# The end of a fused four-layer kernel: experts merged beside the norms, and half of each tile's experts scaled and added by two other engines

## The reference, cut to what matters

```python
# the closing norm of the fourth cross attention; its result is added to x
out = (out - mu) * jax.lax.rsqrt(var + EPS) * ln_scale + ln_bias      # EPS = 1e-6
x = x + out
# the encoder runs on _layernorm(x), which has no scale of its own
def _moe(x, wg, w1, b1, w2, b2):               # 8 experts, D = 128, FF = 512
    xf = x.reshape(S, D)                       # S = 2048 tokens, cap = S // 8
    gates = jax.nn.softmax(xf @ wg, axis=-1)
    idx = jnp.argmax(gates, axis=-1)
    ... # loc: the token's place among those of its expert; keep = loc < cap
    h = jnp.einsum('ecd,edf->ecf', disp, w1) + b1[:, None, :]
    y = (jnp.einsum('ecf,efd->ecd', h, w2) + b2[:, None, :]).reshape(E * cap, D)
    out = jnp.where(keep[:, None], gate_val[:, None] * y[...], 0.0)
y1 = _ln(x + _mha(x, in_proj_w, in_proj_b, out_proj_w, out_proj_b), ln1_g, ln1_b)
y2 = _ln(y1 + _moe(y1, wg, w1, b1, w2, b2), ln2_g, ln2_b)
x = x + y2                                     # the kernel's output
```

## Time and profile before

| what | value |
|---|---|
| median of three runs | 4094.75 us |
| the profiled execution's own time | 4094.75 us |
| its span in the profile | 4093.0 us |
| PE busy | 3629.6 us (89%) |
| DVE busy | 2716.3 us (66%) |
| ACT busy | 2253.7 us (55%) |
| POOL busy | 1367.2 us (33%) |

### The profile page before, as it was taken

How to read it: one execution, slowest core, us unless ns; L and a number is a source line. 1 busy time by engine, 2 the same in 40 slices (tenths; PEclk the granted TensorE clock), 3 DMA queues, 4 the chain that set the end, 5 groups by cost and what they waited for, 6 DMA issues and landing times. The chain is left out here.

```text
span 4093.0 us, 72451 instructions
## 1 busy us (share of the span) xinstructions
PE 3629.6 (89%) x28012; PEld 2243.5 (55%) x28017; DVE 2716.3 (66%) x4497; ACT 2253.7 (55%) x3885; POOL 1367.2 (33%) x1655
## 2 busy tenths in 40 slices
PE   3699999889699986997889999999999999999554
PEld 2233333478444434675457776777677776776441
DVE  5799999644477736554347666666666666766648
ACT  2599999633277752222146566665666566656220
POOL 3011111230011102210035556655565556556310
PEclk7699999999799986998989999999999999999777
DMA  4422232001256401000010000000000000000010
GB/s 140 130 59 54 49 58 48 21 12 36 65 78 92 67 2 31 2 2 10 12 53 17 1 1 17 1 17 1 17 1 17 1 17 1 1 1 1 7 42 16
DMA packets 117717, 122.90 MB, mean 30 GB/s; under 512 B 19008, under 2 KB 95648, under 8 KB 116992
## 3 DMA queue, kind: packets, MB, share of 16 engines
q1 hardware_dynamic: 104184, 111.20, 12.0%
q10 hardware_dynamic: 13200, 7.16, 0.6%
HBM read 102.51 MB, written 15.68 MB: 29 GB/s over the span
## 5 line engine op out<-in xcount | busy, mean ns | idle before, releaser
L869 DVE TENSOR_REDUCE att_peak.1<-psS 128x1 f32<-128x512 f32 (+1 forms) x1024 | 579.1, 633 | 21.0 <-PE psS L744 14.7
L2098 DVE TENSOR_TENSOR att_highest.1<-att_highest.1,psS 128x1024 f32<-128x1024 f32 (+1 forms) x320 | 356.7, 1115 | 218.1 <-ACT prob_0.1 L2032 111.8
L839 ACT ACTIVATE att_probT.1<-psT 128x512 f32<-128x512 f32 (+1 forms) x682 | 366.6, 568 | 29.6 <-PE psT L773 9.6
L2190 POOL TENSOR_TENSOR key_sums_0.1<-key_sums_0.1,prob_0.1 128x512 f32<-128x512 f32 x256 | 334.5, 1306 | 28.7 <-POOL key_sums_0.1 L2190 0.4
L2190 POOL TENSOR_TENSOR key_sums_1.1<-key_sums_1.1,prob_1.1 128x512 f32<-128x512 f32 x256 | 332.3, 1298 | 32.8 <-ACT prob_1.1 L2038 5.1
L869 DVE TENSOR_REDUCE att_peak.2<-psS 128x1 f32<-128x512 f32 (+1 forms) x512 | 261.7, 568 | 79.1 <-PE psS L744 76.2
L790 PE MATMUL psM<-att_probT.1,quad_values.1 128*9 128x256 f32 (+1 forms) x3840 | 292.6, 382 | 0.2 <-issue 0.2
L744 PE MATMUL psS<-key_stack.1,query_stack.1 64*128 64x512 bf16 (+1 forms) x1024 | 253.6, 379 | 25.0 <-PEq L379 15.9
L2110 DVE TENSOR_REDUCE att_shift.4<-psO 128x4 f32<-128x512 f32 x64 | 44.3, 692 | 319.0 <-PE psO L1941 319.0
L2185 POOL TENSOR_TENSOR key_sums_0.1<-prob_0.1 128x512 f32<-128x512 f32 x64 | 81.8, 1277 | 517.2 <-ACT prob_0.1 L2038 517.2
L2119 DVE TENSOR_TENSOR prob_1.1<-prob_1.1,psO 128x1024 f32<-128x1024 f32 (+1 forms) x256 | 245.7, 1012 | 5.6 <-PE psO L1948 5.6
(11 more groups left out here) (687 smaller groups left out, 7857.2 us busy)
## 6 DMA issues: line engine op xcount, KB each, us to landing
key_stack.1<-key_parts SPq DMA_DIRECT2D x384, 58.0 KB
key_stack.2<-key_parts SPq DMA_DIRECT2D x96, 200.1 KB
ctx_rows.1<-in_ctx_dram SPq DMA_DIRECT2D x8, 1536.0 KB
key_parts<-split_parts.2 SPq DMA_DIRECT2D x8, 1200.8 KB, 7.4
ctx_keys_0.1<-in_ctx_dram ACTq DMA_DIRECT2D x4, 768.0 KB
ctx_keys_1.1<-in_ctx_dram ACTq DMA_DIRECT2D x4, 768.0 KB
query_stack.1<-query_parts SPq DMA_DIRECT2D x192, 16.0 KB
ctx_values_0.1<-in_ctx_dram SPq DMA_DIRECT2D x4, 768.0 KB
```

Of the source, the lines that this page charges most:

```text
L839: self.k.nc.scalar.activation(probs[:, blks[0]:blks[-1] + 1, :].rearrange("p b q -> p (b q)"), bank[0:w, 0:len(blks) * S], ACT.Exp).then_i ...
L869: self.k.nc.vector.tensor_reduce(self.peak[:, 2 * h + s, c:c + 1], self.score_bank[m % 3][:, 0:w], AX_X, ALU.max).then_inc(self.peak_done. ...
L2098: self.k.nc.vector.tensor_tensor(own, old, new, ALU.max).then_inc(self.raised.sem, 1)
L2190: nc.gpsimd.tensor_tensor(acc, acc, own[:, h, c * BANK:(c + 1) * BANK], ALU.add).then_inc(self.summed.sem, 1)
```

## The change

The new code is in seven parts.

- `MergedExperts` keeps all weights of the eight experts in buffers of their own and the merged result in `both[P, E, 2, D]`: for each expert the matrix and its bias row. The bias row gets `b2` by a matmul with a row of ones, and the bias product is the same on every partition.
- `two_norms_beside_experts` joins the closing norm of the cross attention, its scale and shift, and the norm ahead of the encoder in one block. DVE goes by groups of four tiles. SP issues the loads of the experts (25 DMAs) and those of scale and shift, ACT the eleven others, and PE, ACT and POOL merge experts 0 to 3.
- `norm_beside_experts` does ln1, its scale and shift, and the transposes in one block, and merges experts 4 to 7 on the other engines; on PE they stand ahead of the transposes.
- The blocks `load` and the loop over the experts are gone; `softmax_gates` and `place_in_order` stay.
- `apply_experts` adds the bias rows on PE, by a matmul with one row of contraction (the ones times the bias rows) into the same PSUM bank. DVE takes experts 0 to 3 straight from PSUM. ACT scales experts 4 to 7 by the token's weight into a ring of three buffers, POOL adds the four to one, and DVE adds that one two tiles later and takes the tile's statistics for ln2 at once.
- `last_norm` does the rest of ln2 by groups of four tiles, and SP stores each group (256 KB).
- `scale_and_shift`, `transpose_tokens`, `single_expert` and `store` are gone.

```diff
+def dve_scale_and_shift(k, link, norm, g, scale, shift):
+    for t in range(4 * g, 4 * g + 4):
+        last = norm.dve_apply(t)
+    link(last)
+    x = four_tiles(k.XN, g)
+    link(k.nc.vector.tensor_tensor(x, x, over_four(scale), ALU.mult))
+    return k.nc.vector.tensor_tensor(x, x, over_four(shift), ALU.add)
...
+    def pe_run(self, pe, first, end):            # MergedExperts
+        self.pe_turn(pe, first)                  # 4 transposes of w1
+        for e in range(first, end):
+            if e + 1 < end:
+                self.pe_turn(pe, e + 1)
+            self.pe_product(pe, e)               # 4 + 4 + 1 matmuls
...
+        @block.sync                              # two_norms_beside_experts
+        def _(sp):
+            for e in range(2):
+                experts.load(sp, e)
+            for dst, src in ((scale, "L3_xattn_ln_scale"), (shift, "L3_xattn_ln_bias")):
+                sp.dma_start(dst[:], rows(k.dram[src])).then_inc(affine_loaded.sem, 16)
+            for e in range(2, E):
+                experts.load(sp, e)
+            sp.wait_ge(*loaded(16 * len(loads)))
...
+            old.dve_invert(dve, link)
+            dve.wait_ge(*affine_loaded(32))
+            for g in range(NT // 4):
+                link(dve_scale_and_shift(k, link, old, g, scale, shift))
+                x = four_tiles(k.X, g)
+                link(nc.vector.tensor_tensor(x, x, four_tiles(k.XN, g), ALU.add))
+                for t in range(4 * g, 4 * g + 4):
+                    last = new.dve_stats(t)
...
+        def _(pe):                               # norm_beside_experts
+            experts.pe_run(pe, EARLY, E)         # EARLY = 4
+            for g in range(NT // 4):
+                pe.wait_ge(*xn_done(g + 1))
+                turn_tiles(k, pe, g, xt_done)
...
-                for i in range(HALF):            # apply_experts, PE
-                    n = t * HALF + i
-                    if n >= 4:
-                        pe.wait_ge(*biased(n - 3))
-                    nc.tensor.matmul(k.psS[:, n % 4, :], k.XT[:, t * P:(t + 1) * P], w12[:, i * BANK:(i + 1) * BANK],
-                                     start=True, stop=True).then_inc(product.sem, 1)
+                for i in range(2):
+                    if t >= 2 and i == 0:
+                        pe.wait_ge(*added(added_at(t - 2)))
+                    if t >= 2 and i == 1:
+                        pe.wait_ge(*scaled(EB * (t - 1)))
+                    own = slice(EB * i, EB * i + EB)
+                    out = k.psS[:, 2 * i + t % 2, :].rearrange("p (e d) -> p e d", d=D)
+                    nc.tensor.matmul(out, k.XT[:, t * P:(t + 1) * P], experts.both[:, own, 0, :], start=True, stop=False)
+                    nc.tensor.matmul(out, experts.ones[:], experts.both[0:1, own, 1, :], start=False, stop=True).then_inc(product[i].sem, 1)
+        @block.scalar
+                for e in range(EB):              # EB = 4
+                    nc.scalar.activation(y[:, t % 3, e, :], k.psS[:, 2 + t % 2, e * D:(e + 1) * D], ACT.Identity,
+                                         scale=comb[:, t, EB + e:EB + e + 1]).then_inc(scaled.sem, 1)
+        @block.gpsimd
+                nc.gpsimd.tensor_tensor(part[:, t % 3], y[:, t % 3, 0:EB // 2], y[:, t % 3, EB // 2:EB], ALU.add).then_inc(halved.sem, 1)
+                pool.wait_ge(*halved(t + 1))
+                nc.gpsimd.tensor_tensor(part[:, t % 3, 0], part[:, t % 3, 0], part[:, t % 3, 1], ALU.add).then_inc(pooled.sem, 1)
+        @block.vector
+            def take_part(t, at):
+                x = k.XN[:, t, :]
+                dve.wait_ge(*pooled(t + 1))
+                dve.wait_ge(*added(at))
+                nc.vector.tensor_tensor(x, x, part[:, t % 3, 0], ALU.add).then_inc(added.sem, 1)
+                dve.wait_ge(*added(at + 1))
+                return norm.dve_stats(t)
...
-            sp.dma_start(k.out.rearrange("b (t p) d -> p (b t) d", p=P), k.X[:]).then_inc(stored.sem, 16)
+            for g in range(GROUPS):              # last_norm, GROUPS = 4
+                sp.wait_ge(*ready(g + 1))
+                sp.dma_start(four_tiles(out, g), four_tiles(k.X, g)).then_inc(stored.sem, 16)
```

More of the change, by code:

```diff
@@ L2255, in scale_and_shift, with last_norm @@
+def last_norm(k, norm, scale, shift):
+    nc, chain, ready, stored = k.nc, k.flag("dve_chain"), k.flag("x_added"), k.flag("stored")
+    GROUPS = NT // 4
     with nc.Block() as block:
@@ L2258, in _ @@
             link = Chain(dve, chain)
[L2260 to L2265, removed]
-            link.end()
[L2269 to L2278, removed]
+            norm.dve_variance(dve, link)
@@ L2280, in _ @@
+            norm.dve_invert(dve, link)
+            for g in range(GROUPS):
+                link(dve_scale_and_shift(k, link, norm, g, scale, shift))
+                x = four_tiles(k.X, g)
+                nc.vector.tensor_tensor(x, x, four_tiles(k.XN, g), ALU.add).then_inc(ready.sem, 1)
+            link.end()
         @block.scalar
         def _(act):
-            for g in range(NT // 4):
-                act.wait_ge(*xt_done(g + 1))
-                nc.scalar.copy(k.XT[:, g * BANK:(g + 1) * BANK], k.psS[:, g, :]).then_inc(xt_copied.sem, 1)
@@ L2285, in transpose_tokens @@
[L2285 to L2299, removed]
@@ L2304, in batch_attention, with _ @@
-def batch_attention(k, loads):
+            norm.act_deviation(act)
+        @block.sync
+        def _(sp):
+            out = k.out.rearrange("b (t p) d -> p (b t) d", p=P)
+            for g in range(GROUPS):
+                sp.wait_ge(*ready(g + 1))
+                sp.dma_start(four_tiles(out, g), four_tiles(k.X, g)).then_inc(stored.sem, 16)
+            sp.wait_ge(*stored(16 * GROUPS))
+def batch_attention(k, experts, loads):
     nc = k.nc
@@ L2673, in _ @@
+            at = 0
+            for t in range(NT):
+                x = k.XN[:, t, :]
+                dve.wait_ge(*product[0](t + 1))
+                for e in range(EB):
                     if e >= 1:
[L2674 to L2676 removed]
+                        dve.wait_ge(*added(at))
+                    nc.vector.scalar_tensor_tensor(out=x, in0=k.psS[:, t % 2, e * D:(e + 1) * D], scalar=comb[:, t, e:e + 1], in1=x,
@@ L2677, in _ @@
                                                    op0=ALU.mult, op1=ALU.add).then_inc(added.sem, 1)
-    product.passed(NT * HALF)
-    biased.passed(NT * HALF)
-    added.passed(NT * E)
+                    at += 1
+                if t >= 2:
+                    take_part(t - 2, at)
+                    at += 1
+            for t in range(NT - 2, NT):
+                last = take_part(t, at)
+                at += 1
+            last.then_inc(norm.stat_done.sem, 1)
+            dve.wait_ge(*norm.stat_done(1))
@@ L2683, in experts_beside_choice @@
+    for sig in product:
+        sig.passed(NT)
+    for sig in (halved, pooled):
+        sig.passed(NT)
+    scaled.passed(EB * NT)
+    added.passed(PER * NT)
 def experts_beside_choice(k, mem, gates, comb, ws, bs, power, weights, w1, w2, b1, b2, att):
```

325 lines of the change are left out of this document (226 added, 99 removed).

## The result

The changed kernel is slower, by 0.4%: 4110.71 us, the median of eight runs (4108.44 to 4118.68), for 4094.22 of the kernel before. The ratio is 1.004, with a 95% interval of 1.003 to 1.0049. The forecast was 4038.0, between 4029 and 4053. The profiled execution has a span of 4108.2, 15.2 more than before.

A forecast was written before the change was run, and what follows sets the result against it. DVE bounded the applying before and PE was to bound it after; 2.7 - 2.8 - 3.9 - 0.5 - 37.9 - 9.7 - 4.6 = -56.7 from a span of 4093.0, plus 1.75 around it, gave 4038.0 us, range 4029 to 4053.

The forecast's parts named there:

- A, first norms: Joined first norms beside experts 0 to 3: later start of the applying and narrower instructions, +2.7 (0.5 to 6).
- B, the attention: Attention: same instructions and 60.0, its clock phase shifting by up to 2 either way.
- C and D: ln1 beside experts 4 to 7: XT earlier, -2.8; blocks that go: load -3.9, gates' matmuls -0.5, expert loop -37.9.
- Rivals 1 and 5: PE slow merging experts 4 to 7, +7.5, 12%; merging in the first norms late, up to +6, 6%.
- E, the applying: Applying the experts: PE bounds at 128 x 0.43 = 55.0, with slow start and tail 60.6 for 70.3, -9.7.
- Rival 4: Slower than before: PE at 1.2 GHz through the applying, waiting for DVE and ACT to free banks; 4100, 3%.
- F, the last norm: Last norm: statistics taken in the applying, groups of four tiles, smaller last store, -4.6 (-3 to -5.5).

## Why the prediction was wrong, step by step

- **A, first norms: forecast +2.7, measured +5.4.** From the statistics to the first copy behind the norms: 3865.80 - 3831.09 = 34.7, before 3862.04 - 3832.68 = 29.4. The applying of the norm started 8.9 after the statistics instead of 5.3, with both waits that were named, the root and then the shift row: +3.6 for the +2.4 taken. A load of 256 KB took 4.5 from issue to landing in the median, for 2.8 before, with more loads at once on both queues. The rest are the twelve instructions of 512 columns, one every 0.73 and not 0.67, and one of them of 1.09. (The terms of the sum add up to +2.6, not +2.7, and ACT's loads are 0.64 MB, not 0.58.)
- **B, the attention:** +0.5, forecast 0 within 2.
- **C and D: forecast -45.1, measured -45.0.** XT was there 17.3 after ln1's statistics instead of 19.4 (-2.0, forecast -2.8), with PE at a clock of 0.90 and through its experts before the last group, as taken. The loads gave -4.1, the gates -1.0, the loop -37.9. Rivals 1 and 5 didn't come.
- **E, the applying: forecast -9.7, measured +61.3. This step failed,** in the one term 128 x 0.43 = 55.0: it was 128 x 1.00 = 128.3. Of the 73.3 over, 55 are the half clock, 128 x 0.43 once more, and 18 the emptying, 64 x 0.29. Its form was right, PE as the bound, the counts of DVE and ACT, the tail; so was its reading that a one-row matmul lasts as long as a 128-row one. With the bias matmul at 128 rows the stage took 60.5 where the step gave 60.6, and the kernel 4037.8 where the sum gave 4038.0. That the totals meet so closely is luck: in that run's own profile steps A and B are 3.4 over their forecasts (+4.6 and +1.5), and its four executions lie between 4033.9 and 4043.6. What was wrong is that the row count has no effect on the pace. I took the duration of a 32-row record from a stretch in which all have 32 rows, and carried it to one in which the rows alternate; that brings the emptying, 0.29 a matmul. And I took the clock to follow busy time alone.
- The evidence on the clock was in the trace of before, 22 us behind the row that I read. This is the same line one pass later, with PE's windows over it:

```profile
1530.64 4.78 PE L1232 MATMUL psS<-net_3.1,cn_w_columns.1 32*128 32x512 f32 x8
```

```profile
1530.00:1532.00 2.00, 2.00 (x5) 0.66 (x4) 0.00 (x0) 1.80 (x3) 0.00 (x0) 1.00 0.00 0
1532.00:1534.00 2.00, 2.00 (x5) 0.89 (x4) 0.54 (x2) 1.99 (x4) 0.00 (x0) 0.78 0.00 0
```

  Eight 32-row records take 4.78 and not 3.69, and the clock falls in the midst of them, with PE busy 2.00 of 2.00. Only matmuls of 64 and 32 rows were at work there since 1527.0. In the pass before, the same rows kept the clock at 1.00 until PE paused. Of this fall I had only a window from 1532 to 1536, at 0.64 with PE busy 3.62 of 4.00, and took nothing from it.
- **Rival 4** had the half clock and the right sign, at 3%, but for a cause that wasn't there: PE paused for nobody. Its 128 x 0.86 also lacked the emptying; its sum of 4100 came near only because C and A were added at their worst. (Its +51 takes the slow start off twice; 110 - 57.0 is +53.)
- **F, the last norm: forecast -4.6, measured -5.3.** The last store ended 2.7 behind the last addition's end (4108.2 for 4105.5). The steps A to F add up to +16.8; the span grew by 15.2, since the part ahead of the change, with the same code, took 1.6 less.
- **What the named change is worth.** In step E the split between DVE, ACT and POOL was said to take work out of the bound without setting the pace. Two pairs of runs show it: nothing clear of the scatter with a 128-row float32 bias on PE (ratio 0.9856 with, 0.9868 without), 17 where the bias is cheap (4016.5 and 4033.5).

## What to carry to other kernels

Adding a row vector with a one-row matmul behind each full one costs as much PE time as the full matmul and here 0.2 to 0.3 us more for each change of rows, and it also kept PE at 1.2 GHz; give it 128 rows (a block of 1/128 against rows that are equal on all partitions, or bfloat16 parts). Grouping the one-row matmuls, full ones first, gained nearly as much here. Before taking a duration or a clock from another stage, look at every pass of that stage and at whether its neighbours have the same shape. Before moving work off an engine, count whether the engine that feeds it leaves room: the split gained nothing measurable until PE had.

## What the runs showed of the hardware

- A change of contraction rows between matmuls cost 0.19 us at 2.4 GHz and 0.29 at 1.2 GHz for 1, 32 and 64 rows against 128; 96 rows against 128 cost nothing.
- With 128-row and one-row matmuls by turns, and PE busy without a gap for 128 us by the profile, the granted clock stayed at 0.50; entered at 1.00, it fell to 0.50 after about 8 us of them. With 32 or 64 rows by turns it stayed at 0.50 when entered there, and at 1.00 when entered there.
- With full rows and twice as much emptying it rose from 0.50 to 1.00.
- A change between float32 and bfloat16 matmuls of 128 rows cost nothing (0.86 for the float32 pair, 0.21 for the bfloat16 record, at 2.4 GHz).
